# Plain additions for the softmax shift, and x loaded a second time in 32-channel pieces and transposed by VectorE instead of TensorE

## The chip, the core and the metric

The kernel runs on one core of a Trainium2 chip. The time is that of one execution on the device, in microseconds (us), the median of the executions shown. TensorE (PE) multiplies matrices out of SBUF into PSUM, VectorE (DVE), ScalarE (ACT) and GpSimd (POOL) work on 128 partitions by so many elements, and SyncE (SP) issues the transfers between memory and SBUF. Each engine runs its own instructions strictly in order; between engines, and where one instruction of an engine reads what the one before it wrote, there are semaphores.

## The reference

Self-attention over the W axis of an image tensor, after a normalisation with fixed mean and variance, everything in float32, B, H, W, C = 64, 128, 128, 64:

```
xn = (x - moving_mean) * rsqrt(moving_var + 0.001) * gamma + beta
q = xn @ Wq + bq;  k = xn @ Wk + bk;  v = xn @ Wv + bv
scores = einsum('bhid,bhjd->bhij', q, k) * 64 ** -0.5
attn = softmax(scores, axis=-1)
out = einsum('bhij,bhjd->bhid', attn, v) @ Wo + bo
return xn + out
```

There are 64 x 128 = 8192 rows of the image, each an attention of its own over 128 tokens of 64 channels.

## The kernel before

Eight image rows are a group; there are 1024 groups. The weights and the normalisation are folded once, at the start, into one 64x64 matrix for the scores (`w_g`), one for the output (`w_o`), a row of weights (`row_weights`, two rows of 64: one that scales x, one that gives the part of the score that depends on the query alone) and some biases (`const_bias` is one number per partition).

For each group n the work goes as follows, and the names are those of the tiles:

- SP loads x into `x_in` (128 tokens by 8 rows by 64 channels, 256 KB). There are eight buffers.
- PE transposes x (four 128x128 transposes into `ux_ps`, line 498) and DVE copies the result to `xT` (line 409), with channels of two image rows on the partitions. PE multiplies it with `w_g` (`g_ps`, line 483), ACT adds the bias (`g`, line 271), and PE makes the scores (`score_ps`, line 456).
- POOL multiplies x with `row_weights` into `x_weighted` (line 231, 128x1024), which has two buffers, and adds a bias to one half of it: `x_scaled_rows` (line 236).
- DVE sums the other half of `x_weighted` over the channels (`row_const`, 8 numbers per partition, line 401). This is what lets POOL write its next `x_weighted` but one: POOL waits on `const_found` (n - 2).
- DVE finds the largest score of each row (`row_max`, line 376), then `top` = `row_const` + `const_bias` + `row_max` (line 392) and `neg_top` = `row_const` + `const_bias` - `top` (line 395), 8 numbers per partition each. Both use an instruction with two tiles and one per-partition number (SCALAR_TENSOR_TENSOR). ACT takes `neg_top` as the bias of the eight exponentials (`probs`, line 287).
- PE transposes `probs` in two halves (line 443), ACT copies them (`probsT`, lines 264 and 277), PE multiplies x with them (into `ux_ps`, the same PSUM bank as the x transposes, line 467), DVE copies that to `uT` (line 385), PE multiplies by `w_o` (`o_ps`, line 508), and DVE multiplies with one over the sum of the exponentials (`inv_sum` line 365, `attn` line 370).
- POOL adds `attn` and `x_scaled_rows` (`y`, line 245) and SP stores `y`.

The work is pipelined by hand. In step t each engine takes different groups, always in the same written order:

- DVE: `inv_sum` and `attn` of group t-3, `row_max` of t, `uT` of t-2, `top` and `neg_top` of t, `row_const` of t+1, `xT` of t+2.
- POOL: `x_weighted` and `x_scaled_rows` of t+2, `y` of t-3.
- PE: scores of t, the product with x of t-2, first half of the transposed `probs` of t-1, `g_ps` of t+1, second half, the x transposes of t+2, `o_ps` of t-2.
- SP: the load of t+4, the store of t-3.

POOL's wait, in its step for group n = t+2, is this:

```
if exists(r, n - 2, peeled):
    pool.wait_ge(const_found[parts(n - 2)], uses(r, n - 2))
    pool.wait_ge(x_scaled[parts(n - 2)], uses(r, n - 2))
```

The steady part is a loop of eight steps per turn (`Fori`), with 19 steps written out ahead of it and 12 behind it.

Of the kernel before, what the change touches and what calls it, by code (L numbers as in the profile page):

```python
# [6 lines left out]
ALU = mybir.AluOpType  # L7
# [10 lines left out]
def build(nc: bass.Bass, x, gamma, beta, mean, var, wq, bq, wk, bk, wv, bv, wo, bo, out):  # L18
# [7 lines left out]
    x_groups = x.rearrange("b h w c -> (b h) w c").rearrange("(g s) w c -> g w s c", s=GROUP)  # L26
    out_groups = out.rearrange("b h w c -> (b h) w c").rearrange("(g s) w c -> g w s c", s=GROUP)

    with ExitStack() as ctx:
# [13 lines left out]
        x_in = sb("x_in", [128, 8, GROUP, C])  # L43
        xT = sb("xT", [128, 4, PAIRS, W])
        g = sb("g", [128, 4, PAIRS, W])
        x_weighted = sb("x_weighted", [128, 2, GROUP, 2, C])
        x_scaled_rows = sb("x_scaled_rows", [128, 8, GROUP, C])
        row_const = sb("row_const", [128, 4, GROUP])
# [36 lines left out]
        ux_ps, g_ps, probsT_ps, o_ps = (psum(n) for n in ("ux_ps", "g_ps", "probsT_ps", "o_ps"))  # L85
        score_ps = [psum(f"score_ps{i}", (128, 2, 512)) for i in range(2)]

        x_loaded = sem_ring("x_loaded", 8)
        y_stored = sem_ring("y_stored")
        xT_made = sem_ring("xT_made")  # L90
# [11 lines left out]
        neg_top_found = sem_ring("neg_top_found")  # L102
        const_found = sem_ring("const_found")
# [20 lines left out]
        class Turn:  # L124


            def __init__(self, eng, r, dma):
                self.r = r
                self.uses = {k: eng.snap(r * 2 + k) for k in range(-2, 5)}
                self.dma = {k: eng.snap((r * 2 + k) * DMA_INC) for k in range(-2, 5)} if dma else {}  # L130
                self.dma8 = {k: eng.snap((r + k) * DMA_INC) for k in range(0, 3)} if dma else {}
# [5 lines left out]
        def dma_uses(r, n):  # L137
            k = n // SEMS + 1
            return DMA_INC * (2 * r + k) if isinstance(r, int) else r.dma[k]

# [26 lines left out]
        def _(sp):  # L167
# [16 lines left out]

            def store(r, n, peeled):
# [4 lines left out]

            load(0, 0, True)

            def step(r, t, peeled):
                load(r, t + 4, peeled)
                store(r, t - 3, peeled)
# [15 lines left out]
        def _(pool):  # L211
# [38 lines left out]
        def _(act):  # L250
# [6 lines left out]
            def step(r, t, peeled):  # L257
# [21 lines left out]
                if exists(r, n, peeled):  # L279
# [6 lines left out]
                    for q in range(GROUP):  # L286
                        last = nc.scalar.activation(probs[:, n % 2, q, :], score_ps[n % 2][:, q % 2, q // 2 * W:(q // 2 + 1) * W],  # L287
# [9 lines left out]
        def _(dve):  # L297
# [50 lines left out]
            for h in range(2):  # L348
                p = slice(h * C, (h + 1) * C)
                chain(nc.vector.tensor_copy(w_g[p, h, :], ux_ps[p, 0:C]))  # L350
                chain(nc.vector.tensor_copy(w_o[p, h, :], ux_ps[p, C:2 * C]))
            chain(nc.vector.tensor_copy(row_weights[:, 1, :], ux_ps[:, 2 * C:3 * C]))
            chain(nc.vector.tensor_tensor(out_bias[:], ux_ps[:, 3 * C:4 * C], b_row[:], ALU.add))
            chain(nc.vector.tensor_copy(g_bias[:], ux_ps[:, 4 * C:4 * C + 1]))
            chain(nc.vector.tensor_copy(const_bias[:], ux_ps[:, 4 * C + 1:4 * C + 2]))
# [4 lines left out]
            def step(r, t, peeled):  # L360
# [12 lines left out]
                if exists(r, n, peeled):  # L373
                    s = parts(n)
                    dve.wait_ge(scores_made[s], uses(r, n))
                    nc.vector.tensor_reduce(row_max[:, s, :].rearrange("p (k h) -> p h k", h=2),  # L376
# [3 lines left out]
                if exists(r, n, peeled):  # L380
# [4 lines left out]
                    nc.vector.tensor_copy(uT[:, n % 2], ux_ps[:].rearrange("p (k w) -> p k w", k=PAIRS)) \  # L385
                        .then_inc(u_kept[s], 1)
                n = t
                if exists(r, n, peeled):
# [23 lines left out]
            pipeline(dve, step)  # L412

        @block.tensor
        def _(pe):
# [12 lines left out]
            for o, lhsT, rhs in ((0, wqT, w_foldT[:, 1, 0, :]),  # L428
# [5 lines left out]
                last = nc.tensor.matmul(ux_ps[:, o:o + rhs.shape[1]], lhsT, rhs, start=True, stop=True)  # L434
# [4 lines left out]
            w_o_all = w_o[:].rearrange("p h c -> p (h c)")  # L439

# [5 lines left out]
            def step(r, t, peeled):  # L446
# [13 lines left out]
                if exists(r, n, peeled):  # L460
                    s = parts(n)
                    pe.wait_ge(probsT_b_kept[s], uses(r, n))
                    if exists(r, n + 3, peeled):
                        pe.wait_ge(xT_kept[parts(n + 3)], uses(r, n + 3))
                    for k in range(PAIRS):
                        for h in range(2):
                            last = nc.tensor.matmul(ux_ps[h * C:(h + 1) * C, k * W:(k + 1) * W], x_in[:, n % 8, 2 * k + h, :],  # L467
                                                    probsT[:, n % 2, 2 * k + h, :], start=True, stop=True)
# [22 lines left out]
                n = t + 2  # L491
                if exists(r, n, peeled):
                    s = parts(n)
                    pe.wait_ge(x_loaded[n % 8], load_uses(r, n))
# [38 lines left out]
```

## Time and profile before

| | us |
|---|---|
| median of 3 executions | 5887.01 (5886.72 to 5887.08) |
| the profiled execution, its own time | 5891.6 |
| its span in the trace | 5889.8 |

| engine | busy us | share of the span |
|---|---|---|
| DVE | 5769.4 | 98% |
| PE | 5650.5 | 96% |
| POOL | 4992.3 | 85% |
| ACT | 4783.0 | 81% |
| the 16 DMA engines, mean | | 41.6% |

TensorE's granted clock is 0.999 of full speed over the span. An instruction counts as busy from its start to its end in the trace, whatever it does or waits for in between; idle time ahead of an instruction is shown apart, with what released it. In the timeline a row gives start, duration, engine, line, operation, output and inputs, and in brackets the idle time ahead of it.

### The profile page before, as it was taken

How to read it: one execution, taken by the hardware profiler on the slowest of the kernel's cores; microseconds unless marked ns; L12 is line 12 of the kernel's file. 1: busy time of each engine (PE TensorE's matmuls, PEld its weight loads, DVE VectorE, ACT ScalarE, POOL GpSimd, SP SyncE). 2: the span in 40 equal slices, each digit the busy share in tenths (PEclk: the TensorE clock that was granted, in tenths of full speed). 3: DMA queues.
4: the chain of work that ended last, by engine and by line, in shares of the span. 5: the costliest groups of instructions: out<-in, count | busy, mean ns of one | idle time of the engine just before them, and what ended most of it. 6: DMA issues, size and time to landing. Idle time of an engine off the chain costs nothing.

```text
span 5889.8 us, 169868 instructions
## 1 busy us (share of the span) xinstructions
PE 5650.5 (96%) x55320; PEld 4441.6 (75%) x55320; DVE 5769.4 (98%) x8226; ACT 4783.0 (81%) x19460; POOL 4992.3 (85%) x3080
## 2 busy tenths in 40 slices
PE   7999999999999999999999999999999999999999
PEld 6777777777777777777777777777777777777777
DVE  8999999999999999999999999999999999999999
ACT  6888888888888888888888888888888888888887
POOL 7888888888888888888888888888888888888887
PEclk9999999999999999999999999999999999999999
DMA  3444444444444444444444444444444444444443
GB/s 76 91 93 93 92 91 91 93 93 91 91 92 93 93 91 91 93 93 92 91 91 93 93 91 91 92 93 93 91 91 92 93 92 91 91 93 93 91 91 85
DMA packets 2131546, 537.56 MB, mean 91 GB/s; under 512 B 2131520, under 2 KB 2131520, under 8 KB 2131520
## 3 DMA queue, kind: packets, MB, share of 16 engines
q1 hardware_dynamic: 2131520, 537.23, 41.6%
q8 instruction: 14, 0.23, 0.0%
q14 instruction: 12, 0.10, 0.0%
HBM read 268.67 MB, written 268.44 MB: 91 GB/s over the span
## 4 chain that ended last, share of the span: by engine, by line
PE 68%; DVE 23%; issue 8%; DVEq 1%; POOL 0%; SPq 0%; ACT 0%; DMA 0%; POOLq 0%
PE probsT_ps L443 17%; PE ux_ps L467 17%; PE o_ps L508 14%; PE g_ps L483 13%; DVE xT L409 11%; DVE row_const L401 8%; PE ux_ps L498 7%; DVE top L392 2%; DVE uT L385 1%; DVE row_max L376 1%; DVEq L369 1%; DVEq L156 0%; DVE inv_sum L365 0%; PE score_ps L456 0%; POOL y L245 0%
## 5 line engine op out<-in xcount | busy, mean ns | idle before, releaser
L287 ACT ACTIVATE probs<-score_ps,neg_top 128x128 f32<-128x128 f32 x8192 | 2874.9, 376 | 686.1 <-DVE neg_top L395 686.1
L231 POOL TENSOR_TENSOR x_weighted<-x_in,row_weights 128x1024 f32<-128x1024 f32 x1024 | 2427.1, 2370 | 789.1 <-issue 675.9
L287 ACT ACTIVATION_READ_ACCUMULATOR probs<-score_ps,neg_top 128x1 f32 x8192 | 1765.5, 216 | 0.0
L443 PEld LDWEIGHTS probsT_ps<-ident,probs 128*128 128x128 f32 x8192 | 859.0, 140 | 915.0 <-issue 727.4
L236 POOL TENSOR_TENSOR x_scaled_rows<-x_weighted,out_bias 128x512 f32<-128x512 f32 x1024 | 1307.4, 1277 | 90.8 <-POOL x_weighted L231 20.2
L443 PE MATMUL probsT_ps<-ident,probs 128*128 128x128 f32 x8192 | 1315.5, 283 | 5.9 <-ACT probs L287 3.7
L467 PE MATMUL ux_ps<-probsT,x_in 128*64 128x128 f32 x16384 | 1120.8, 278 | 203.1 <-DVE xT L409 176.7
L245 POOL TENSOR_TENSOR y<-attn,x_scaled_rows 128x512 f32<-128x512 f32 x1024 | 1301.6, 1271 | 13.8 <-DVE attn L370 13.8
L395 DVE SCALAR_TENSOR_TENSOR neg_top<-row_const,const_bias,top 128x8 f32<-128x8 f32 x1024 | 1217.1, 1189 | 36.3
L376 DVE TENSOR_REDUCE row_max<-score_ps 128x8 f32<-128x1024 f32 x1024 | 1243.4, 1214 | 2.2 <-PE score_ps L456 2.0
L456 PE MATMUL score_ps<-xT,g 64*128 64x128 f32 x16384 | 1190.0, 285 | 0.3 <-ACT g L271 0.3
L467 PEld LDWEIGHTS ux_ps<-probsT,x_in 128*64 128x64 f32 x16384 | 895.9, 136 | 376.2 <-issue 300.9
L456 PEld LDWEIGHTS score_ps<-xT,g 64*128 64x128 f32 x16384 | 993.9, 187 | 124.2 <-ACT g L271 1.1
L508 PE MATMUL o_ps<-w_o,uT 128*128 128x128 f32 x8192 | 1082.1, 275 | 0.8 <-DVE uT L385 0.8
L483 PE MATMUL g_ps<-xT,w_g 128*128 128x512 f32 x2048 | 1050.3, 595 | 0.9 <-DVE xT L409 0.9
L508 PEld LDWEIGHTS o_ps<-w_o,uT 128*128 128x128 f32 x8192 | 995.3, 192 | 1.0 <-DVE uT L385 1.0
L271 ACT ACTIVATE g<-g_ps,g_bias 128x512 f32<-128x512 f32 x1024 | 703.8, 687 | 290.4 <-PE g_ps L483 290.3
L392 DVE SCALAR_TENSOR_TENSOR top<-row_const,const_bias,row_max 128x8 f32<-128x8 f32 x1024 | 816.6, 798 | 0.1
L370 DVE TENSOR_TENSOR attn<-o_ps,inv_sum 128x512 f32<-128x512 f32 x1024 | 707.9, 691 | 53.0 <-issue 5.7
L264 ACT ACTIVATE probsT<-probsT_ps 128x512 f32<-128x512 f32 x1024 | 611.5, 597 | 107.3 <-PE probsT_ps L443 3.0
L385 DVE COPY uT<-ux_ps 128x512 f32<-128x512 f32 x1024 | 696.8, 680 | 0.6 <-PE ux_ps L467 0.6
L409 DVE COPY xT<-ux_ps 128x512 f32<-128x512 f32 x1024 | 690.8, 675 | 3.8 <-PE ux_ps L498 3.8
(66 smaller groups left out, 2908.1 us busy)
## 6 DMA issues: line engine op xcount, KB each, us to landing
x_in<-in_x SPq DMA_DIRECT2D x1024, 256.0 KB, 3.2
out<-y SPq DMA_DIRECT2D x1024, 256.0 KB, 2.8
norm_row<-in_L_conv_gamma SPq DMA_DIRECT2D x1, 32.0 KB, 3.7
norm_row<-in_L_conv_beta SPq DMA_DIRECT2D x1, 32.0 KB, 3.7
norm_row<-in_L_conv_moving_mean SPq DMA_DIRECT2D x1, 32.0 KB, 4.2
norm_row<-in_L_conv_moving_var SPq DMA_DIRECT2D x1, 32.0 KB, 4.3
norm_row<-in_L_conv_bo SPq DMA_DIRECT2D x1, 32.0 KB, 4.5
w_raw<-in_L_conv_Wq SPq DMA_DIRECT2D x1, 16.0 KB, 1.9
```

The lines of the kernel that those rows point to most:

```text
L231: nc.gpsimd.tensor_tensor(x_weighted[:, n % 2], x_in[:, n % 8, :, None, :].broadcast_to([128, GROUP, 2, C]), weights_b, ALU.mult).then_inc ...
L236: nc.gpsimd.tensor_tensor(x_scaled_rows[:, n % 8], x_weighted[:, n % 2, :, 0, :], bias_b, ALU.add).then_inc(x_scaled[s], 1)
L245: nc.gpsimd.tensor_tensor(y[:, s], attn[:, s], x_scaled_rows[:, n % 8], ALU.add).then_inc(y_found[s], 1)
L287: last = nc.scalar.activation(probs[:, n % 2, q, :], score_ps[n % 2][:, q % 2, q // 2 * W:(q // 2 + 1) * W], ACT.Exp, bias=neg_top[:, s, q ...
L376: nc.vector.tensor_reduce(row_max[:, s, :].rearrange("p (k h) -> p h k", h=2), score_ps[n % 2][:].rearrange("p h (k w) -> p h k w", k=PAIR ...
L395: nc.vector.scalar_tensor_tensor(neg_top[:, s, :], row_const[:, s, :], const_bias[:, 0:1], top[:, s, :], ALU.add, ALU.subtract).then_inc(n ...
L409: nc.vector.tensor_copy(xT[:, s], ux_ps[:].rearrange("p (k w) -> p k w", k=PAIRS)) \
L443: last = nc.tensor.transpose(probsT_ps[:, (q - first) * W:(q - first + 1) * W], probs[:, n % 2, q, :], ident[:])
L456: last = nc.tensor.matmul(score_ps[n % 2][:, h, k * W:(k + 1) * W], g[half, s, k, :], xT[half, s, k, :], start=True, stop=True)
L467: last = nc.tensor.matmul(ux_ps[h * C:(h + 1) * C, k * W:(k + 1) * W], x_in[:, n % 8, 2 * k + h, :], probsT[:, n % 2, 2 * k + h, :], start ...
L483: nc.tensor.matmul(g_ps[:], w_g_all, xT[:, s].rearrange("p k w -> p (k w)"), start=True, stop=True).then_inc(g_made[s], 1)
L508: last = nc.tensor.matmul(o_ps[:, k * 2 * C:(k + 1) * 2 * C], uT[:, n % 2, k, :], w_o_all, start=True, stop=True)
```

## The change

Three things are changed together.

1. `top` and `neg_top` become plain additions of two tiles. For this `const_bias` is added beforehand: DVE's sum over the channels now writes `row_part`, and a new DVE instruction, at the end of the step, makes `row_const` = `row_part` + `const_bias` (8 numbers per partition). POOL now waits on `row_part` (`part_found`), where it waited on `row_const`.
2. x is read from memory a second time. For each group SP issues four more transfers, each of 32 partitions with 16 runs of 32 channels (128 bytes) per partition, 64 KB each, into a new tile `x_quads`. They go ahead of the load of `x_in`.
3. DVE transposes `x_quads` in 32x32 blocks into `xT`, in the place where it copied `xT` out of PSUM. The four x transposes on PE and their waits go away; the PSUM bank is now used by the product with x alone (`u_ps`). The pairs of rows that share a tile are now (k, k+4) in place of (2k, 2k+1), so the order of indices on PE, ACT and DVE's `row_max` changes with it.

```diff
 POOL, step for n = t + 2:
-                        pool.wait_ge(const_found[parts(n - 2)], uses(r, n - 2))
+                        pool.wait_ge(part_found[parts(n - 2)], uses(r, n - 2))

 SP:
+            def load_quads(r, n, peeled):
+                if not exists(r, n, peeled):
+                    return
+                s = parts(n)
+                if exists(r, n - 4, peeled):
+                    sp.wait_ge(xT_kept[s], uses(r, n - 4))
+                for h in range(2):
+                    for a in range(2):
+                        q = 32 * (2 * h + a)
+                        sp.dma_start(x_quads[q:q + 32, s].rearrange("p k (b c) -> p (k b) c", c=32),
+                                     x_blocks[group(r, n), h, a]).then_inc(quads_loaded[s], DMA_INC)
...
             def step(r, t, peeled):
+                load_quads(r, t + 4, peeled)
                 load(r, t + 4, peeled)
                 store(r, t - 3, peeled)

 DVE, step:
-                    nc.vector.scalar_tensor_tensor(top[:, s, :], row_const[:, s, :], const_bias[:, 0:1], row_max[:, s, :],
-                                                   ALU.add, ALU.add).then_inc(top_found[s], 1)
+                    nc.vector.tensor_tensor(top[:, s, :], row_const[:, s, :], row_max[:, s, :],
+                                            ALU.add).then_inc(top_found[s], 1)
                     dve.wait_ge(top_found[s], uses(r, n))
-                    nc.vector.scalar_tensor_tensor(neg_top[:, s, :], row_const[:, s, :], const_bias[:, 0:1], top[:, s, :],
-                                                   ALU.add, ALU.subtract).then_inc(neg_top_found[s], 1)
+                    nc.vector.tensor_tensor(neg_top[:, s, :], row_const[:, s, :], top[:, s, :],
+                                            ALU.subtract).then_inc(neg_top_found[s], 1)
                 n = t + 1
...
                     dve.wait_ge(x_weighed[s], uses(r, n))
-                    nc.vector.tensor_reduce(row_const[:, s, :], x_weighted[:, n % 2, :, 1, :],
-                                            AX_X, ALU.add).then_inc(const_found[s], 1)
+                    nc.vector.tensor_reduce(row_part[:, s, :], x_weighted[:, n % 2, :, 1, :],
+                                            AX_X, ALU.add).then_inc(part_found[s], 1)
                 n = t + 2
...
-                    dve.wait_ge(xT_made[s], uses(r, n))
+                    dve.wait_ge(quads_loaded[s], quad_uses(r, n))
                     if exists(r, n - 4, peeled):
                         dve.wait_ge(scores_made[s], uses(r, n - 4))
-                    nc.vector.tensor_copy(xT[:, s], ux_ps[:].rearrange("p (k w) -> p k w", k=PAIRS)) \
-                        .then_inc(xT_kept[s], 1)
+                    nc.vector.transpose(xT[:, s].rearrange("p k w -> p (k w)"),
+                                        x_quads[:, s].rearrange("p k w -> p (k w)")).then_inc(xT_kept[s], 1)
+                n = t + 1
+                if exists(r, n, peeled):
+                    s = parts(n)
+                    dve.wait_ge(part_found[s], uses(r, n))
+                    nc.vector.tensor_tensor(row_const[:, s, :], row_part[:, s, :], const_bias[:, 0:1].broadcast_to([128, GROUP]),
+                                            ALU.add).then_inc(const_found[s], 1)

 PE, product with x of t - 2, and the x transposes:
-                    if exists(r, n + 3, peeled):
-                        pe.wait_ge(xT_kept[parts(n + 3)], uses(r, n + 3))
+                    if exists(r, n - 1, peeled):
+                        pe.wait_ge(u_kept[parts(n - 1)], uses(r, n - 1))
...
-                    for k in range(PAIRS):
-                        last = nc.tensor.transpose(ux_ps[:, k * W:(k + 1) * W],
-                                                   x_in[:, n % 8, 2 * k:2 * k + 2, :].rearrange("p s c -> p (s c)"), ident[:])
-                    last.then_inc(xT_made[s], 1)
```

The order of instructions on VectorE, one step of the steady part, before (from `row_const` to `neg_top`; sizes are partitions by elements):

```order
L401 TENSOR_REDUCE row_const<-x_weighted 128x8
L409 COPY xT<-ux_ps 128x512
L365 RECIPROCAL inv_sum<-prob_sum 128x8
L370 TENSOR_TENSOR attn<-o_ps,inv_sum 128x512
L376 TENSOR_REDUCE row_max<-score_ps 128x2x4
L385 COPY uT<-ux_ps 128x512
L392 SCALAR_TENSOR_TENSOR top<-row_const,const_bias,row_max 128x8
L395 SCALAR_TENSOR_TENSOR neg_top<-row_const,const_bias,top 128x8
```

And the same place after the change:

```order
L425 TENSOR_REDUCE row_part<-x_weighted 128x8
L433 STREAM_TRANSPOSE xT<-x_quads 128x512
L439 TENSOR_TENSOR row_const<-row_part,const_bias 128x8
L389 RECIPROCAL inv_sum<-prob_sum 128x8
L394 TENSOR_TENSOR attn<-o_ps,inv_sum 128x512
L400 TENSOR_REDUCE row_max<-score_ps 128x8
L409 COPY uT<-u_ps 128x512
L416 TENSOR_TENSOR top<-row_const,row_max 128x8
L419 TENSOR_TENSOR neg_top<-row_const,top 128x8
```

The step has nine instructions where it had eight: `row_const` is now a small instruction of its own behind the transpose, and ahead of `inv_sum`.

On TensorE the same step, before:

```order
L456 MATMUL score_ps<-xT,g 128x128 x8
L467 MATMUL ux_ps<-probsT,x_in 64x128 x8
L443 MATMUL probsT_ps<-ident,probs 128x128 x4
L483 MATMUL g_ps<-xT,w_g 128x512
L443 MATMUL probsT_ps<-ident,probs 128x128 x4
L498 MATMUL ux_ps<-ident,x_in 128x128 x4
L508 MATMUL o_ps<-w_o,uT 128x128 x4
```

And after:

```order
L488 MATMUL score_ps<-xT,g 128x128 x8
L499 MATMUL u_ps<-probsT,x_in 64x128 x8
L475 MATMUL probsT_ps<-ident,probs 128x128 x4
L515 MATMUL g_ps<-xT,w_g 128x512
L475 MATMUL probsT_ps<-ident,probs 128x128 x4
L530 MATMUL o_ps<-w_o,uT 128x2x64 x4
```

Only the x transposes are gone; `o_ps` is written as two runs of 64.

## Rows read from the trace of the kernel before

**Rows 1.** The page: busy time by engine, and POOL's first group with its idle time.

```profile
PE 5650.5 (96%) x55320; PEld 4441.6 (75%) x55320; DVE 5769.4 (98%) x8226; ACT 4783.0 (81%) x19460; POOL 4992.3 (85%) x3080
...
L231 POOL TENSOR_TENSOR x_weighted<-x_in,row_weights 128x1024 f32<-128x1024 f32 x1024 | 2427.1, 2370 | 789.1 <-issue 675.9
```

**Rows 2.** The timeline of one steady step, VectorE and GpSimd: start, duration, engine.

```profile
3005.75 0.67 DVE L401 TENSOR_REDUCE row_const<-x_weighted 128x8 f32<-128x512 f32 x1
...
3006.35 0.68 DVE L409 COPY xT<-ux_ps 128x512 f32<-128x512 f32 x1
...
3006.56 2.37 POOL L231 TENSOR_TENSOR x_weighted<-x_in,row_weights 128x1024 f32<-128x1024 f32 x1 [0.75 <-issue]
...
3006.95 0.19 DVE L365 RECIPROCAL inv_sum<-prob_sum 128x8 f32<-128x8 f32 x1
...
3007.17 0.69 DVE L370 TENSOR_TENSOR attn<-o_ps,inv_sum 128x512 f32<-128x512 f32 x1
...
3007.78 1.21 DVE L376 TENSOR_REDUCE row_max<-score_ps 128x8 f32<-128x1024 f32 x1
...
3008.91 0.68 DVE L385 COPY uT<-ux_ps 128x512 f32<-128x512 f32 x1
3009.00 1.27 POOL L236 TENSOR_TENSOR x_scaled_rows<-x_weighted,out_bias 128x512 f32<-128x512 f32 x1
3009.50 0.80 DVE L392 SCALAR_TENSOR_TENSOR top<-row_const,const_bias,row_max 128x8 f32<-128x8 f32 x1
...
3010.23 1.27 POOL L245 TENSOR_TENSOR y<-attn,x_scaled_rows 128x512 f32<-128x512 f32 x1
...
3010.34 1.19 DVE L395 SCALAR_TENSOR_TENSOR neg_top<-row_const,const_bias,top 128x8 f32<-128x8 f32 x1
...
3011.45 0.67 DVE L401 TENSOR_REDUCE row_const<-x_weighted 128x8 f32<-128x512 f32 x1
```

**Rows 3.** Lines 395 and 392 alone: ns min/median/max, first and last start.

```profile
L395 DVE SCALAR_TENSOR_TENSOR neg_top<-row_const,const_bias,top x1024: 227/1192/1310, 37.1 to 5875.1; 128x8 f32<-128x8 f32 x171
...
L392 DVE SCALAR_TENSOR_TENSOR top<-row_const,const_bias,row_max x1024: 217/802/2254, 34.8 to 5874.8; 128x8 f32<-128x8 f32 x171
```

**Rows 4.** The timeline of the first steps, around the first `top`.

```profile
34.70 2.35 POOL L231 TENSOR_TENSOR x_weighted<-x_in,row_weights 128x1024 f32<-128x1024 f32 x1
...
34.82 2.25 DVE L392 SCALAR_TENSOR_TENSOR top<-row_const,const_bias,row_max 128x8 f32<-128x8 f32 x1
...
37.13 1.26 POOL L236 TENSOR_TENSOR x_scaled_rows<-x_weighted,out_bias 128x512 f32<-128x512 f32 x1
```

**Rows 5.** The timeline of the last steps; GpSimd's next row after this `y` starts at 5872.81.

```profile
5868.74 1.26 POOL L245 TENSOR_TENSOR y<-attn,x_scaled_rows 128x512 f32<-128x512 f32 x1 [2.13 <-DVE attn L370]
...
5870.30 0.22 DVE L392 SCALAR_TENSOR_TENSOR top<-row_const,const_bias,row_max 128x8 f32<-128x8 f32 x1
...
5870.56 0.23 DVE L395 SCALAR_TENSOR_TENSOR neg_top<-row_const,const_bias,top 128x8 f32<-128x8 f32 x1
5870.70 0.68 DVE L401 TENSOR_REDUCE row_const<-x_weighted 128x8 f32<-128x512 f32 x1
```

**Rows 6.** The timeline of the same steady step as Rows 2, TensorE.

```profile
3007.17 1.09 PE L467 MATMUL ux_ps<-probsT,x_in 128*64 128x128 f32 x16 [0.23 <-DVE xT L409]
...
3010.10 0.60 PE L498 MATMUL ux_ps<-ident,x_in 128*128 128x128 f32 x4
...
3010.53 1.06 PE L508 MATMUL o_ps<-w_o,uT 128*128 128x128 f32 x8
```

**Rows 7.** The page on transfers: packets and bytes, then the queue's share of 16 engines.

```profile
DMA packets 2131546, 537.56 MB, mean 91 GB/s; under 512 B 2131520, under 2 KB 2131520, under 8 KB 2131520
...
q1 hardware_dynamic: 2131520, 537.23, 41.6%
```

**Rows 8.** The timeline of SP at the start: the first eight loads, issued in a burst.

```profile
10.16 9.06 SPq L183 DMA_DIRECT2D x_in<-in_x  x8
```

**Rows 9.** Who waited for whom, SP: us in total, times, longest.

```profile
SPq L189 <- POOL y L245: 4591.6, 1024, 34.1
```

More of the change, by code:

```diff
@@ L43, in build @@
         x_in = sb("x_in", [128, 8, GROUP, C])
+        x_quads = sb("x_quads", [128, 4, PAIRS, W])
         xT = sb("xT", [128, 4, PAIRS, W])
@@ L47, in build @@
         x_scaled_rows = sb("x_scaled_rows", [128, 8, GROUP, C])
+        row_part = sb("row_part", [128, 4, GROUP])
         row_const = sb("row_const", [128, 4, GROUP])
@@ L81, in build @@
         row_tmp = sb("row_tmp", [128, 3, C])
-        ux_ps, g_ps, probsT_ps, o_ps = (psum(n) for n in ("ux_ps", "g_ps", "probsT_ps", "o_ps"))
+        u_ps, g_ps, probsT_ps, o_ps = (psum(n) for n in ("u_ps", "g_ps", "probsT_ps", "o_ps"))
         score_ps = [psum(f"score_ps{i}", (128, 2, 512)) for i in range(2)]
         x_loaded = sem_ring("x_loaded", 8)
+        quads_loaded = sem_ring("quads_loaded")
         y_stored = sem_ring("y_stored")
-        xT_made = sem_ring("xT_made")
         g_made = sem_ring("g_made")
@@ L130, in __init__ @@
                 self.dma = {k: eng.snap((r * 2 + k) * DMA_INC) for k in range(-2, 5)} if dma else {}
+                self.quads = {k: eng.snap((r * 2 + k) * 4 * DMA_INC) for k in range(-2, 5)} if dma else {}
                 self.dma8 = {k: eng.snap((r + k) * DMA_INC) for k in range(0, 3)} if dma else {}
@@ L139, in dma_uses, with quad_uses @@
             return DMA_INC * (2 * r + k) if isinstance(r, int) else r.dma[k]
+        def quad_uses(r, n):
+            k = n // SEMS + 1
+            return 4 * DMA_INC * (2 * r + k) if isinstance(r, int) else r.quads[k]
         def load_uses(r, n):
@@ L349, in _ @@
                 p = slice(h * C, (h + 1) * C)
[L350 to L355, printed above, removed]
+                chain(nc.vector.tensor_copy(w_g[p, h, :], u_ps[p, 0:C]))
+                chain(nc.vector.tensor_copy(w_o[p, h, :], u_ps[p, C:2 * C]))
+            chain(nc.vector.tensor_copy(row_weights[:, 1, :], u_ps[:, 2 * C:3 * C]))
+            chain(nc.vector.tensor_tensor(out_bias[:], u_ps[:, 3 * C:4 * C], b_row[:], ALU.add))
+            chain(nc.vector.tensor_copy(g_bias[:], u_ps[:, 4 * C:4 * C + 1]))
+            chain(nc.vector.tensor_copy(const_bias[:], u_ps[:, 4 * C + 1:4 * C + 2]))
             assert done[0] == DVE_READY, done[0]
@@ L375, in step @@
                     dve.wait_ge(scores_made[s], uses(r, n))
-                    nc.vector.tensor_reduce(row_max[:, s, :].rearrange("p (k h) -> p h k", h=2),
+                    nc.vector.tensor_reduce(row_max[:, s, :].rearrange("p (h k) -> p h k", h=2),
                                             score_ps[n % 2][:].rearrange("p h (k w) -> p h k w", k=PAIRS),
@@ L433, in _ @@
                                  (4 * C + 1, bias_wide[:, 0, :], bias_fold[:, 1:2])):
-                last = nc.tensor.matmul(ux_ps[:, o:o + rhs.shape[1]], lhsT, rhs, start=True, stop=True)
+                last = nc.tensor.matmul(u_ps[:, o:o + rhs.shape[1]], lhsT, rhs, start=True, stop=True)
             last.then_inc(pe_setup, 1)
@@ L439, in _ @@
             w_o_all = w_o[:].rearrange("p h c -> p (h c)")
+            o_pairs = o_ps[:].rearrange("p (h k c) -> p h k c", h=2, k=PAIRS)
             def transposed_probs(n, first):
@@ L462, in step @@
                     pe.wait_ge(probsT_b_kept[s], uses(r, n))
-                    if exists(r, n + 3, peeled):
-                        pe.wait_ge(xT_kept[parts(n + 3)], uses(r, n + 3))
+                    if exists(r, n - 1, peeled):
+                        pe.wait_ge(u_kept[parts(n - 1)], uses(r, n - 1))
                     for k in range(PAIRS):
                         for h in range(2):
-                            last = nc.tensor.matmul(ux_ps[h * C:(h + 1) * C, k * W:(k + 1) * W], x_in[:, n % 8, 2 * k + h, :],
-                                                    probsT[:, n % 2, 2 * k + h, :], start=True, stop=True)
+                            last = nc.tensor.matmul(u_ps[h * C:(h + 1) * C, k * W:(k + 1) * W], x_in[:, n % 8, PAIRS * h + k, :],
+                                                    probsT[:, n % 2, PAIRS * h + k, :], start=True, stop=True)
                     last.then_inc(u_made[s], 1)
@@ L507, in step @@
                     for k in range(PAIRS):
-                        last = nc.tensor.matmul(o_ps[:, k * 2 * C:(k + 1) * 2 * C], uT[:, n % 2, k, :], w_o_all,
+                        last = nc.tensor.matmul(o_pairs[:, :, k, :], uT[:, n % 2, k, :], w_o_all,
                                                 start=True, stop=True)
```

15 lines of the change are left out of this document (6 added, 9 removed).

## The prediction

> **What bounds the kernel now.** The page first: DVE 98% and PE 96% busy, POOL 85% [rows 1]. That reads as a VectorE bound, but POOL sat idle 789.1 us ahead of `x_weighted`, 0.77 us in each of 1024 steps, always in the same place. So I read one steady step of DVE and POOL side by side [rows 2].
>
> `x_weighted` starts at 3006.56, 0.14 us after `row_const` has ended (3006.42). `x_scaled_rows` follows at 3009.00 and `y` at 3010.23, ending at 3011.50. And DVE's `top`, 8 numbers per partition, takes 0.80 us and ends at 3010.30, where `x_scaled_rows` ends (3010.27); `neg_top` takes 1.19 us and ends at 3011.53, where `y` ends (3011.50). Over all steps they took 217 to 2254 and 227 to 1310 ns [rows 3]. Where POOL is idle they take 0.22 and 0.23 us [rows 5]. The very first `top` met a just started `x_weighted`: begun 0.12 us after it, it ended at 37.07, that instruction at 37.05 [rows 4]. So a DVE instruction that reads two SBUF tiles waits until the POOL instruction in progress has ended; it gets through at the boundary between two. Instructions with one SBUF input don't: `row_const`, `inv_sum`, `attn` (its other input is PSUM) and `uT` run at their usual length beside POOL's.
>
> That closes a loop: `row_const` lets POOL start; three POOL instructions follow; `y` holds `neg_top`, and `row_const` of the next step is queued behind `neg_top`. With T the start of `row_const`: x_weighted +0.81, x_scaled_rows +3.25, y +4.48 to +5.75, next `row_const` +5.70 [rows 2]. The mean over the kernel, first to last `neg_top`, is (5875.1 - 37.1) / 1023 = 5.707 us [rows 3]. PE is not in this loop: it waits 0.23 us for DVE's `xT` in that step [rows 6].
>
> **The change, part by part**, on that clock, T now being the start of `row_part`.
>
> *POOL's release.* `row_part` is the same reduction in the same place, and POOL now waits on it. `x_weighted` again starts at +0.81 and ends at +3.18 (2.37 long). The release is not moved.
>
> *The transpose* starts at +0.60 like the copy did. The trace has no such instruction. Nearest rows: the sum over the same 128x512 out of SBUF, 0.67 us, and the copy of 128x512, 0.68 us. I take 0.68; below, nothing suggests under 0.3; above, four passes over the data would be 2.7. Up to about 2.4 us it costs nothing, because of what comes next.
>
> *The new addition* reads `row_part` and `const_bias`, both in SBUF, and is DVE's third instruction of that kind in a step. It would start at +1.20 (+0.60 + 0.60), inside `x_weighted` (+0.81 to +3.18). By [rows 4] it waits to the end: done at +3.21, and what follows on DVE starts at +3.13 (0.08 before the end, as `row_const` did behind `neg_top` in [rows 2]). What is queued behind it: `inv_sum`, `attn`, `row_max`, `uT`, `top`. The Trainium skill, page "SBUF — State Buffer", section "Who interferes with whom", states that a DVE instruction with two SBUF inputs contends with a GpSimd instruction that reads SBUF, and that plain tensor_tensor does too; this speaks against the change, since by it plain additions gain nothing and a third is one more wait. The trace agrees for the three-operand form (0.80 and 1.19 us against 0.22); for plain additions no row beside POOL shows it.
>
> *The rest of DVE's step*, by the distances between starts in [rows 2]: `inv_sum` +3.13, `attn` +3.35, `row_max` +3.96, `uT` +5.09, `top` +5.68. POOL meanwhile: `x_scaled_rows` +3.25, `y` +4.48 to +5.75 (`attn` is ready at +4.04). `top` meets the last 0.07 us of `y` and ends at +5.78; `neg_top` starts 0.04 later, +5.82, as in [rows 2]. POOL is idle, since it waits for the next `row_part`, so `neg_top` is short, and `row_part` starts 0.14 behind its start [rows 5]: **+5.96**.
>
> So the loop becomes `row_part`, `x_weighted`, the addition, and the whole of DVE's step, in place of POOL's three instructions. The waits of `top` and `neg_top` (0.58 and 0.96 us over 0.22) nearly vanish, and one of 1.9 us comes ahead of them.
>
> *PE* loses the x transposes, 0.43 us from their start to `o_ps` [rows 6]. It needs 5.70 - 0.23 - 0.43 = 5.04 us a step, below 5.96: no gain in time. Splitting `o_ps` into runs and the new pairs move no instruction; nothing.
>
> *Transfers.* 2048 packets of 256 bytes a step now; the first eight loads went out at 1.13 us each (9.06 / 8) [rows 8], so load and store need 2.3 us. The quads are 4 x 32 x 16 = 2048 packets of 128 bytes: 1.1 us if bytes count, 2.3 if packets do. Together 3.4 to 4.6 us of a 5.96 us step. The share of the DMA engines goes from 41.6% [rows 7] to between 60 and 80%. SP waits 4591.6 us of the span for `y` [rows 9] and has room for four more issues; the loads are asked for some three steps ahead. Cost nothing, as long as a step's packets stay below the step.
>
> **The sum.** (5.96 - 5.70) x 1023 = +266 us. The profiled execution's own time was 5891.6, 1.8 us more than its span of 5889.8 us; the median of the runs is 5887.0, 2.8 below that span. Span after: 6156; median: **6153 us**, 4.5% more. Its own uncertainty: `top` reaches POOL's `y` with 0.07 us to spare. If DVE is earlier nothing changes; if it is later by d, the loop grows by about d. With a free `neg_top` of 0.19 (like `inv_sum`) instead of 0.23, 5.92: 6112. With 0.15 us more on DVE, and register work of the loop that no longer hides, 6.15: 6347. Own range 6090 to 6350.
>
> **The rivals.**
>
> *Plain additions don't wait for POOL* (faster). For it: only the three-operand form is seen waiting. Against it: what the two forms have in common is two tiles from SBUF, and `attn`, a plain multiplication with one SBUF tile, never waits. Then DVE's step is 0.60 + 0.60 + 0.14 + 0.22 + 0.61 + 1.13 + 0.59 + 0.26 + 0.14 = 4.3, POOL's 4.94 (0.81 to 5.75), PE's 5.04 the longest: -0.66 x 1023, about 5210. It decides if `row_const` takes 0.2 us beside `x_weighted`. Chance 0.11.
>
> *Only the new addition slips through*, because its second operand is one number repeated and may not be fetched as a tile is. DVE then reaches `top` at 0.60 + 0.60 + 0.14 + 0.22 + 0.61 + 1.13 + 0.59 = +3.89, waits for `x_scaled_rows` to +4.55, `neg_top` for `y` to +5.78, and `row_part` starts at +5.70: the old loop to the last digit, 5887. Chance 0.09.
>
> *The transfers become the bound* (slower still). If a 128-byte packet cost twice a 256-byte one, 2.27 + 4.53 = 6.8 us a step, 5887 + 1.1 x 1023 = 7010. It decides from 29 ns a packet and engine ((5.96 - 2.27) x 16 / 2048) against 17.7 in the burst. For it: every packet is under 512 bytes already and these are smaller, scattered in memory; against: nothing in [rows 7] shows a price per byte missing. The Trainium skill, "DMA: Bandwidth & Descriptors", section "Why small descriptors are slow (HBM only)", gives a fixed cost per packet, 256/32 + 3 = 11 cycles at 256 bytes, so 7 at 128: by it the quads would take 7/11 of 2.27, an estimate of 1.4 us a step, and this rival would be out. Chance 0.05.
>
> **How the numbers follow.** The wait of the addition behind `x_weighted`: 0.75, and of that about 0.65 within 6090 to 6350. A range from 5870 to 6400 takes in the unchanged loop and leaves out the fast case and the transfers: about 0.8. Within 0.2% of before is about all that a measurement can tell from no change; faster 0.11, same 0.09, slower 0.80.
>
> **What would show it.** The new `row_const` near 1.9 to 2.0 us, ending with `x_weighted`; `top` near 0.1 to 0.3 and `neg_top` near 0.2 us; POOL idle about 1.0 us before each `x_weighted`; PE's share near 85%; DVE still near 98%; the transpose anywhere under 2.4 us without effect; the DMA share 60 to 80%. The prediction is wrong if `row_const` is short beside `x_weighted`, if DVE waits for `x_quads`, if the transpose exceeds 2.4 us, or if POOL's instructions themselves change length.

## The result

The changed kernel takes **6139.8 us** (median of 4, 6139.61 to 6140.16) against 5886.9 us before: ratio 1.043, 95% interval 1.042 to 1.044. It is slower by 253 us; 6153 us was forecast, and 6090 to 6350 as the forecast case's own range.

The page of the kernel after, busy time by engine and GpSimd's first group (beside [rows 1]):

```profile
span 6137.9 us, 172723 instructions
## 1 busy us (share of the span) xinstructions
PE 5404.5 (88%) x51224; PEld 4001.7 (65%) x51224; DVE 6021.7 (98%) x9250; ACT 4792.0 (78%) x19460; POOL 4974.4 (81%) x3080
...
L255 POOL TENSOR_TENSOR x_weighted<-x_in,row_weights 128x1024 f32<-128x1024 f32 x1024 | 2415.6, 2359 | 1054.5 <-issue 909.1
```

DVE is again 98% busy and PE is less so. GpSimd sits idle longer ahead of `x_weighted`, 1054.5 us against 789.1: 265 us more. GpSimd's own instructions took 18 us less in total (4974.4 against 4992.3), so the whole loss stands in this idle time.

The timeline of one steady step after, VectorE and GpSimd (beside [rows 2]):

```profile
3005.62 0.68 DVE L425 TENSOR_REDUCE row_part<-x_weighted 128x8 f32<-128x512 f32 x1
3006.22 0.70 DVE L433 STREAM_TRANSPOSE xT<-x_quads 128x512 f32<-128x512 f32 x1
...
3006.43 2.36 POOL L255 TENSOR_TENSOR x_weighted<-x_in,row_weights 128x1024 f32<-128x1024 f32 x1 [1.01 <-issue]
...
3006.84 1.97 DVE L439 TENSOR_TENSOR row_const<-row_part,const_bias 128x8 f32<-128x8 f32 x1
...
3008.74 0.19 DVE L389 RECIPROCAL inv_sum<-prob_sum 128x8 f32<-128x8 f32 x1
3008.87 1.27 POOL L260 TENSOR_TENSOR x_scaled_rows<-x_weighted,out_bias 128x512 f32<-128x512 f32 x1
3008.96 0.69 DVE L394 TENSOR_TENSOR attn<-o_ps,inv_sum 128x512 f32<-128x512 f32 x1
...
3009.57 1.21 DVE L400 TENSOR_REDUCE row_max<-score_ps 128x8 f32<-128x1024 f32 x1
...
3010.10 1.27 POOL L269 TENSOR_TENSOR y<-attn,x_scaled_rows 128x512 f32<-128x512 f32 x1
...
3010.70 0.68 DVE L409 COPY uT<-u_ps 128x512 f32<-128x512 f32 x1
3011.30 0.16 DVE L416 TENSOR_TENSOR top<-row_const,row_max 128x8 f32<-128x8 f32 x1
...
3011.49 0.17 DVE L419 TENSOR_TENSOR neg_top<-row_const,top 128x8 f32<-128x8 f32 x1
...
3011.57 0.68 DVE L425 TENSOR_REDUCE row_part<-x_weighted 128x8 f32<-128x512 f32 x1
```

From `row_part` to `row_part` it is 5.95 us, where it was 5.70. Read the addition of 8 numbers first: it starts inside `x_weighted`, takes 1.97 us, and ends at 3008.81, where `x_weighted` ends (3008.79). This is not this step alone: 1022 of the 1024 additions start inside an instruction of GpSimd, and each of them ends 19 to 45 ns after it. The other two took 124 and 167 ns. The rest of DVE's step follows the addition, and GpSimd, done with `y` at 3011.37, waits for the next `row_part`. `top` and `neg_top` show no wait any more: GpSimd is idle or just ending when they come.

The groups of VectorE after, mean ns of one after the busy time:

```profile
L439 DVE TENSOR_TENSOR row_const<-row_part,const_bias 128x8 f32<-128x8 f32 x1024 | 2005.9, 1959 | 0.0
...
L433 DVE STREAM_TRANSPOSE xT<-x_quads 128x512 f32<-128x512 f32 x1024 | 717.5, 701 | 0.0
...
L419 DVE TENSOR_TENSOR neg_top<-row_const,top 128x8 f32<-128x8 f32 x1024 | 172.6, 169 | 35.4
L416 DVE TENSOR_TENSOR top<-row_const,row_max 128x8 f32<-128x8 f32 x1024 | 159.6, 156 | 0.1
```

Line 419 alone: ns min/median/max, first and last start.

```profile
L419 DVE TENSOR_TENSOR neg_top<-row_const,top x1024: 166/166/2274, 34.4 to 6123.4; 128x8 f32<-128x8 f32 x171
```

And the transfers on the page after (beside [rows 7]):

```profile
DMA packets 4294236, 806.27 MB, mean 131 GB/s; under 512 B 4294208, under 2 KB 4294208, under 8 KB 4294208
## 3 DMA queue, kind: packets, MB, share of 16 engines
q1 hardware_dynamic: 4294208, 805.93, 65.4%
```

The page's chain, followed back from the last instruction, is VectorE's in the kernel after, and 29% of the span in it is `row_const` (line 439):

```profile
DVE 78%; issue 21%; DVEq 1%; PE 0%; POOL 0%; SPq 0%; DMA 0%; POOLq 0%; ACT 0%; ACTq 0%
```

### The profile page after: what moved, and what is told of

It is laid out like the page before. It is cut to its first block, busy times and chain, and to the rows that moved or that the text cites. A ratio compares the mean times of both kernels' runs of the same rounds, so it can differ in the third digit from the quotient of the medians.

```text
span 6137.9 us, 172723 instructions
## 1 busy us (share of the span) xinstructions
PE 5404.5 (88%) x51224; PEld 4001.7 (65%) x51224; DVE 6021.7 (98%) x9250; ACT 4792.0 (78%) x19460; POOL 4974.4 (81%) x3080
## 3 DMA queue, kind: packets, MB, share of 16 engines
q1 hardware_dynamic: 4294208, 805.93, 65.4%
## 4 chain that ended last, share of the span: by engine, by line
DVE 78%; issue 21%; DVEq 1%; PE 0%; POOL 0%; SPq 0%; DMA 0%; POOLq 0%; ACT 0%; ACTq 0%
DVE row_const L439 29%; DVE row_max L400 20%; DVE uT L409 10%; DVE row_part L425 7%; DVE xT L433 6%; DVE inv_sum L389 2%; DVE top L416 1%; DVE neg_top L419 1%; DVE attn L394 1%; DVEq L415 0%; DVEq L166 0%; POOL y L269 0%; DVEq L393 0%; DMA bias_col<-in_L_conv_bv 0%; PE u_ps L464 0%
## 5 line engine op out<-in xcount | busy, mean ns | idle before, releaser
L255 POOL TENSOR_TENSOR x_weighted<-x_in,row_weights 128x1024 f32<-128x1024 f32 x1024 | 2415.6, 2359 | 1054.5 <-issue 909.1
L439 DVE TENSOR_TENSOR row_const<-row_part,const_bias 128x8 f32<-128x8 f32 x1024 | 2005.9, 1959 | 0.0
L530 PE MATMUL o_ps<-w_o,uT 128*128 128x128 f32 x8192 | 1185.7, 288 | 700.0 <-DVE uT L409 700.0
L499 PE MATMUL u_ps<-probsT,x_in 128*64 128x128 f32 x16384 | 1120.5, 279 | 0.0
L499 PEld LDWEIGHTS u_ps<-probsT,x_in 128*64 128x64 f32 x16384 | 873.3, 136 | 124.1
L433 DVE STREAM_TRANSPOSE xT<-x_quads 128x512 f32<-128x512 f32 x1024 | 717.5, 701 | 0.0
L409 DVE COPY uT<-u_ps 128x512 f32<-128x512 f32 x1024 | 696.1, 680 | 0.6 <-PE u_ps L499 0.6
L425 DVE TENSOR_REDUCE row_part<-x_weighted 128x8 f32<-128x512 f32 x1024 | 694.0, 678 | 1.7 <-POOL x_weighted L255 1.7
```

The source lines that it names most:

```text
L255: nc.gpsimd.tensor_tensor(x_weighted[:, n % 2], x_in[:, n % 8, :, None, :].broadcast_to([128, GROUP, 2, C]), weights_b, ALU.mult).then_inc ...
L409: nc.vector.tensor_copy(uT[:, n % 2], u_ps[:].rearrange("p (k w) -> p k w", k=PAIRS)) \
L425: nc.vector.tensor_reduce(row_part[:, s, :], x_weighted[:, n % 2, :, 1, :], AX_X, ALU.add).then_inc(part_found[s], 1)
L439: nc.vector.tensor_tensor(row_const[:, s, :], row_part[:, s, :], const_bias[:, 0:1].broadcast_to([128, GROUP]), ALU.add).then_inc(const_fo ...
L499: last = nc.tensor.matmul(u_ps[h * C:(h + 1) * C, k * W:(k + 1) * W], x_in[:, n % 8, PAIRS * h + k, :], probsT[:, n % 2, PAIRS * h + k, :] ...
L530: last = nc.tensor.matmul(o_pairs[:, :, k, :], uT[:, n % 2, k, :], w_o_all, start=True, stop=True)
```

## The experiments

Theory, as in the prediction: an instruction of VectorE with two tiles from SBUF waits until GpSimd's instruction in progress has ended, and the new addition stands where that costs about 1.8 us. Rivals: the second load or the transpose costs the time; or VectorE is simply full.

All times are medians. The ratio is to the kernel before, run on the same chip as the kernel of that row; from chip to chip its median lies between 5886.9 and 5890.2 us.

| kernel | us | ratio (95%) |
|---|---|---|
| only the load and the transpose (e1_quads_only) | 5875.7 | 0.998 (0.997 to 0.999) |
| only the additions (e2_adds_only) | 6145.4 | 1.044 (1.042 to 1.046) |
| the new addition ahead of the transpose (e3_add_early) | 5876.7 | 0.998 (0.997 to 0.999) |
| the new addition, one tile and a number (e4_add_scalar) | 6137.9 | 1.043 (1.041 to 1.044) |
| the same with a constant (e8_add_number) | 6137.4 | one run |
| two transposes (e9_two_transposes) | 6143.7 | 1.043 (1.041 to 1.045) |
| five transposes (e10_five_transposes) | 7534.1 | 1.279 (1.277 to 1.281) |
| reductions for additions (e7_pairs) | 5169.9 | 0.878 (0.877 to 0.880) |
| the same, x transposed on PE (e6_pairs_pe) | 5615.6 | 0.954 (0.952 to 0.955) |
| negated row_max, no additions (e5_negmax) | 5170.6 | 0.878 (0.877 to 0.880) |

**Each part alone.** The first kernel is the changed one with the old forms of `top` and `neg_top` and no third addition; `x_weighted` waits for the sum over the channels, as it did before. From its edit against the changed kernel:

```diff
-                    nc.vector.tensor_tensor(top[:, s, :], row_const[:, s, :], row_max[:, s, :],
-                                            ALU.add).then_inc(top_found[s], 1)
+                    nc.vector.scalar_tensor_tensor(top[:, s, :], row_const[:, s, :], const_bias[:, 0:1], row_max[:, s, :],
+                                                   ALU.add, ALU.add).then_inc(top_found[s], 1)
...
-                    nc.vector.tensor_tensor(row_const[:, s, :], row_part[:, s, :], const_bias[:, 0:1].broadcast_to([128, GROUP]),
-                                            ALU.add).then_inc(const_found[s], 1)
...
```

> Only the second load of x and the transpose on VectorE; top, neg_top and row_const are made as before. Theory (the wait of two-input instructions for GpSimd): the loop of row_const, three GpSimd instructions and the held neg_top is untouched, 5.70 us a step, 5887 us within 0.3%, although TensorE loses 0.43 us of work a step; transpose near 0.70 us. Rival (the load or the transpose costs the 4%): near 6140 us.

The second is the kernel before with only the additions changed: `top` and `neg_top` plain, `x_weighted` waiting on `row_part`, and the third addition behind the copy of `xT`. From its edit against the kernel before:

```diff
...
+                    nc.vector.tensor_tensor(row_const[:, s, :], row_part[:, s, :], const_bias[:, 0:1].broadcast_to([128, GROUP]),
+                                            ALU.add).then_inc(const_found[s], 1)
```

> Only the plain additions, with row_const as a third one behind the copy of xT; x is still transposed on TensorE and loaded once. Theory: the third addition waits about 1.97 us for x_weighted, 5.95 us a step, 6120 to 6150 us. Rival (the load or the transpose costs it): 5887 us.

5875.7 and 6145.4 us: the additions cost all of it, and the load, the transpose and PE's relief together cost nothing and give almost nothing. That also settles how to read the page of the kernel before, whose own chain lies mostly on PE:

```profile
PE 68%; DVE 23%; issue 8%; DVEq 1%; POOL 0%; SPq 0%; ACT 0%; DMA 0%; POOLq 0%
```

By that line PE would be the bound; yet with 0.43 us less for PE in each step, 440 us in all, the time fell by 12. The group of the addition in the second kernel:

```profile
L417 DVE TENSOR_TENSOR row_const<-row_part,const_bias 128x8 f32<-128x8 f32 x1024 | 2001.1, 1954 | 0.0
```

It takes the same 1.95 us, about 1.8 of it a wait, with no transpose and no second load there.

**The place of the addition.** In the changed kernel it moves from behind the transpose to directly behind `row_part`; nothing else changes.

```diff
                     nc.vector.tensor_reduce(row_part[:, s, :], x_weighted[:, n % 2, :, 1, :],
                                             AX_X, ALU.add).then_inc(part_found[s], 1)
+                    dve.wait_ge(part_found[s], uses(r, n))
+                    nc.vector.tensor_tensor(row_const[:, s, :], row_part[:, s, :], const_bias[:, 0:1].broadcast_to([128, GROUP]),
+                                            ALU.add).then_inc(const_found[s], 1)
```

> The changed kernel, with the addition that makes row_const moved directly behind row_part, ahead of the transpose. It then starts about 0.10 us before GpSimd's x_weighted. Theory: it slips in ahead (0.15 us), top waits for x_scaled_rows and neg_top for y again, 5.70 to 5.77 us a step, 5885 to 5960 us. If GpSimd is in first all the same, the addition waits for all of x_weighted: 5.95 to 6.05 us a step, 6140 to 6240. Rival (an extra instruction costs what it costs, wherever it stands): 6140 us.

5876.7 us, just under the 5885 to 5960 expected: the whole loss is undone by where the addition stands. The timeline of its steady step:

```profile
3002.07 1.27 POOL L269 TENSOR_TENSOR y<-attn,x_scaled_rows 128x512 f32<-128x512 f32 x1
3002.17 1.19 DVE L419 TENSOR_TENSOR neg_top<-row_const,top 128x8 f32<-128x8 f32 x1
...
3003.29 0.67 DVE L425 TENSOR_REDUCE row_part<-x_weighted 128x8 f32<-128x512 f32 x1
...
3003.99 0.17 DVE L428 TENSOR_TENSOR row_const<-row_part,const_bias 128x8 f32<-128x8 f32 x1
...
3004.09 2.36 POOL L255 TENSOR_TENSOR x_weighted<-x_in,row_weights 128x1024 f32<-128x1024 f32 x1 [0.75 <-issue]
```

It starts 0.10 us ahead of `x_weighted` and takes 0.17 us. The old loop is back: the plain `neg_top` takes 1.19 us and ends with `y` (3003.36 against 3003.34), just as the three-operand one did. The trace of before had no such row, a plain addition with two tiles waiting for GpSimd.

**Which forms wait.** The addition with one tile and a per-partition number, and then with the constant 0.0 in the place of that number (this one leaves `const_bias` out of the sum). The edit of the first:

```diff
-                    nc.vector.tensor_tensor(row_const[:, s, :], row_part[:, s, :], const_bias[:, 0:1].broadcast_to([128, GROUP]),
-                                            ALU.add).then_inc(const_found[s], 1)
+                    nc.vector.tensor_scalar(row_const[:, s, :], row_part[:, s, :], const_bias[:, 0:1], None,
+                                            ALU.add).then_inc(const_found[s], 1)
```

> The changed kernel, with the addition that makes row_const written as one tile plus a per-partition number (tensor_scalar). If only a second tile from SBUF waits for GpSimd: the addition takes 0.15 to 0.2 us, top and neg_top wait in its place, 5.70 us a step, 5880 to 5900 us. If the per-partition number or a faster mode of this instruction needs the shared side as well: 1.97 us, 6140 us.

> The changed kernel with the new addition as one tile plus a constant written in the instruction, 0.0, so const_bias is left out of it. If the per-partition number was what waited for GpSimd in the form with one tile, the addition takes 0.15 to 0.2 us and the time is near 5877; if a tile read and written in SBUF with this instruction is enough, it waits 1.97 us again and the time is near 6138.

6137.9 and 6137.4 us. Its line in the two kernels: ns min/median/max.

```profile
L439 DVE TENSOR_SCALAR row_const<-row_part,const_bias x1024: 186/1977/2336, 30.8 to 6117.2; 128x8 f32<-128x8 f32 x171
```

```profile
L439 DVE TENSOR_SCALAR row_const<-row_part x1024: 129/1977/1986, 30.9 to 6116.8; 128x8 f32<-128x8 f32 x171
```

The wording "two SBUF tiles" was too narrow: this instruction has a single tile from SBUF and writes to SBUF, and waits just the same, with a per-partition number or with a constant. The Trainium skill, "SBUF — State Buffer", section "Who interferes with whom", says that copies and tensor_scalar can enter, when their operands meet certain conditions, a mode that takes both ports into SBUF and then contend with GpSimd. Both runs agree with it (1977 ns), though the mode itself is not seen in a trace. The Trainium skill says in the same section that tensor_reduce on trn2 never contends; the next kernels agree with that (129 to 170 ns).

**No such form at all.** Each small sum becomes a reduction over two neighbouring numbers of one tile. `trio` holds `row_max`, `row_const` and minus `top` side by side; `pair` holds the sum of `x_weighted` and `const_bias`. The arithmetic is the same. From the edit against the changed kernel:

```diff
-                    nc.vector.tensor_tensor(top[:, s, :], row_const[:, s, :], row_max[:, s, :],
-                                            ALU.add).then_inc(top_found[s], 1)
+                    nc.vector.tensor_reduce(trio[:, s, :, 2], trio[:, s, :, 0:2], AX_X, ALU.add, negate=True).then_inc(top_found[s], 1)
...
-                    nc.vector.tensor_tensor(neg_top[:, s, :], row_const[:, s, :], top[:, s, :],
-                                            ALU.subtract).then_inc(neg_top_found[s], 1)
+                    nc.vector.tensor_reduce(neg_top[:, s, :], trio[:, s, :, 1:3], AX_X, ALU.add).then_inc(neg_top_found[s], 1)
...
-                    nc.vector.tensor_tensor(row_const[:, s, :], row_part[:, s, :], const_bias[:, 0:1].broadcast_to([128, GROUP]),
-                                            ALU.add).then_inc(const_found[s], 1)
+                    nc.vector.tensor_reduce(trio[:, s, :, 1], pair[:, s], AX_X, ALU.add).then_inc(const_found[s], 1)
```

> The changed kernel with the same sums, but each small addition is a reduction over two neighbouring numbers of one tile, so that no instruction of VectorE's steady step has two inputs in SBUF. Theory: none of them waits for GpSimd (0.15 to 0.25 us each); the longest engine sets the step, TensorE at about 5.04 us with GpSimd at 4.94 close behind: 5.0 to 5.15 us, 5190 to 5320 us. Rival (these small instructions are slow for another reason than GpSimd, or VectorE is full): 5900 to 6140 us.

> The same reductions over two numbers, but x transposed on TensorE and loaded once, as before the change. Theory: no wait for GpSimd; TensorE, with the x transposes, is the longest engine at 5.47 us: 5640 to 5680 us. The difference to the kernel with the second load is then what taking the x transposes off TensorE is worth, 0.43 us a step or about 440 us. Rival: TensorE was never close to its limit, and both give the same time.

5169.9 us, 12% faster than before; with x transposed on PE and loaded once 5615.6. Both are a little under the lowest that was expected (5190 and 5640): PE's step without waits is 5.00 and 5.44 us, where 5.04 and 5.47 were taken. The page of the first of them, and its groups of VectorE:

```profile
PE 5133.4 (99%) x51224; PEld 3972.6 (77%) x51224; DVE 4239.4 (82%) x9251; ACT 4672.1 (90%) x19460; POOL 4990.8 (97%) x3080
...
q1 hardware_dynamic: 4294208, 805.93, 78.9%
...
PE 99%; issue 0%; DVE 0%; POOL 0%; ACT 0%; SPq 0%; DMA 0%; POOLq 0%; DVEq 0%; ACTq 0%
```

```profile
L417 DVE TENSOR_REDUCE neg_top<-trio 128x8 f32<-128x16 f32 x1024 | 174.1, 170 | 35.6
L415 DVE TENSOR_REDUCE trio<-trio 128x8 f32<-128x16 f32 x1024 | 162.7, 159 | 0.1
L436 DVE TENSOR_REDUCE trio<-pair 128x8 f32<-128x16 f32 x1024 | 132.2, 129 | 0.0
```

And the place of the third sum in its steady step:

```profile
3003.36 2.37 POOL L253 TENSOR_TENSOR x_weighted<-x_in,row_weights 128x1024 f32<-128x1024 f32 x1
...
3003.77 0.13 DVE L436 TENSOR_REDUCE trio<-pair 128x8 f32<-128x16 f32 x1
```

The three sums take 129 to 170 ns each, with GpSimd 97% busy beside them. The third starts 0.41 us into `x_weighted`, just where the addition of the changed kernel started, and is done long before it ends. VectorE falls from 98% busy to 82% with as many instructions in the step; the chain that ended last is 99% PE. The difference between the two kernels, 445.7 us or 0.436 us a step, is PE's time for the x transposes [rows 6]: the second half of the change does pay, once the wait for GpSimd is gone.

**Less work for VectorE.** `neg_top` straight from the reduction, without `top` and without the new addition; the part of the shift that depends on the query alone is left out, since it cancels in the softmax:

```diff
-                    nc.vector.tensor_reduce(row_max[:, s, :].rearrange("p (h k) -> p h k", h=2),
+                    nc.vector.tensor_reduce(neg_top[:, s, :].rearrange("p (h k) -> p h k", h=2),
                                             score_ps[n % 2][:].rearrange("p h (k w) -> p h k w", k=PAIRS),
-                                            AX_X, ALU.max).then_inc(max_found[s], 1)
+                                            AX_X, ALU.max, negate=True).then_inc(neg_top_found[s], 1)
```

> The changed kernel without top and without the new addition: neg_top is the negated row_max, straight from the reduction (the part that depends on the query alone cancels in the softmax; row_part is still summed and still releases GpSimd). VectorE has 0.5 us less to do than with the reductions over two numbers. Theory: TensorE is the limit, so the same time within 1%, 5190 to 5320 us. Rival (VectorE is the limit there): 0.3 to 0.5 us a step less than that kernel.

5170.6 us, the same, and again just under the 5190 expected. VectorE is no bound there; PE is.

**More work for VectorE.** The transpose twice, and five times, the extra ones into a spare tile and ahead of the one into `xT`. The loop of the second kernel; in the first it is `range(1)`:

```diff
+                    for i in range(4):
+                        nc.vector.transpose(spare[:, i, :], x_quads[:, s].rearrange("p k w -> p (k w)"))
```

> The changed kernel with the transpose done a second time, into a spare tile: 0.62 us more for VectorE in each step. Theory: the addition behind it arrives at +1.84 us, still inside x_weighted (+0.81 to +3.17), waits 0.62 us less, and nothing changes: 6140 us within 0.3%. Rival (VectorE, 98% busy, is the bound by its work): 0.62 x 1023 more, 6770 us.

> The transpose five times, four into a spare tile: 2.48 us more for VectorE in each step. Theory: the addition arrives at +3.70 us, after x_weighted and inside x_scaled_rows (+3.25 to +4.52), so it ends at +4.55 in place of +3.20; the step grows by about 1.34 us, to 7.29 us, 7510 us. Had only the time beyond x_weighted's end counted, 0.5 us, 6650. Rival (all of the added work counts): 8.43 us a step, 8680 us.

6143.7 us: 0.62 us of work more in each step, and 4 us in all; the kernel before, too, took 3 us more on that chip (5890.2 against 5886.9), and the ratio is the same 1.043. An engine that is 98% busy had 0.6 us to spare, inside the addition that waits, whose mean fell from 1959 to 1375 ns:

```profile
L444 DVE TENSOR_TENSOR row_const<-row_part,const_bias 128x8 f32<-128x8 f32 x1024 | 1407.8, 1375 | 0.0
```

With five it is 7534.1 us, where following the addition from one instruction of GpSimd to the next gave 7510 and the plain sum of all added work 8680. The timeline:

```profile
3006.34 2.48 DVE L437 STREAM_TRANSPOSE spare<-x_quads 128x512 f32<-128x512 f32 x4
3006.56 2.36 POOL L256 TENSOR_TENSOR x_weighted<-x_in,row_weights 128x1024 f32<-128x1024 f32 x1 [1.39 <-issue]
3008.75 0.67 DVE L438 STREAM_TRANSPOSE xT<-x_quads 128x512 f32<-128x512 f32 x1
3009.00 1.27 POOL L261 TENSOR_TENSOR x_scaled_rows<-x_weighted,out_bias 128x512 f32<-128x512 f32 x1
3009.34 0.95 DVE L444 TENSOR_TENSOR row_const<-row_part,const_bias 128x8 f32<-128x8 f32 x1
...
3011.30 1.26 POOL L270 TENSOR_TENSOR y<-attn,x_scaled_rows 128x512 f32<-128x512 f32 x1 [1.02 <-DVE attn L395]
```

The addition now misses the end of `x_weighted` (3008.92) by 0.42 us, starts 0.34 us into `x_scaled_rows` and waits for its end (3010.27): late by a little, it pays for the rest of the next instruction of GpSimd. The transposes, a tile read and written in SBUF like the tensor_scalar above, don't wait: the four extra ones take 2.48 us together, most of it inside `x_weighted`, and 677 ns each on average over the kernel.

## Why the prediction was right

The time and the mechanism were both right for the change as it was made. One general sentence of the prediction was wrong, and two small errors in the step cancelled; both are below.

- **The loop that bounds the kernel.** Shown. Taking the waits away (the reductions) left PE as the bound, at 5.00 and 5.44 us a step, and DVE's 98% became 82%.
- **The new addition waits behind `x_weighted`.** Forecast to end at +3.21 of the step; it ended at +3.19 (3008.81 - 3005.62). Its place alone carries the loss.
- **What waits, and what doesn't.** "Instructions with one SBUF input don't" was wrong as a rule: the tensor_scalar has one and waits 1.8 us. It did no harm here, since none of DVE's steady instructions before or after the change is of that form. Why some forms wait is not shown by any run. All the waiting instructions had 8 numbers per partition, and all of GpSimd's read SBUF; larger ones, or a GpSimd instruction that only writes, were not tried.
- **The rest of the step.** Forecast `inv_sum` +3.13, `attn` +3.35, `row_max` +3.96, `uT` +5.09, `top` +5.68, next `row_part` +5.96. Measured +3.12, +3.34, +3.95, +5.08, +5.68, +5.95. The forecast had `top` held to the end of `y` and done at +5.78, `neg_top` starting at +5.82, and `row_part` 0.14 behind it. In fact `top` took the 0.16 us that it takes anyway (0.15 in the kernel with five transposes, where GpSimd is idle then) and ended at +5.84, past the end of `y` at +5.75, so no wait shows; `neg_top` started at +5.87, and `row_part` only 0.08 behind it. One error of 0.05 us and one of 0.06 cancelled: that the step came out within 0.01 us is in part luck.
- **The sum.** 253 us for 266. By the first and last `neg_top` the mean step went from 5.707 us to (6123.4 - 34.4) / 1023 = 5.952, so it grew by 0.245 us. The prediction took 0.26, because it subtracted the one step's 5.70 and not its own mean of 5.707, and had 5.96 for 5.952.
- **The transpose.** Taken as 0.68, measured 0.70; free up to about 2.4 us was forecast. Twice the transpose (1.24 us) was free, five times (3.1) was not; where between them it ends was not measured.
- **The transfers.** Forecast share 60 to 80%, measured 65.4%. By share x 16 x span / packets a packet took 18.4 ns of one DMA engine before; the added 2.16 million took (0.654 x 6137.9 - 0.416 x 5889.8) x 16 / 2162688 = 11.6 ns each. Only 2097152 of them are the quads' own packets of 128 bytes; if the others took no time, it is 11.9 ns. Half the bytes cost 0.63 to 0.65 of the time, so that rival was far off: 29 ns would have been needed. The Trainium skill, "DMA: Bandwidth & Descriptors", section "Why small descriptors are slow (HBM only)", has a fixed cost per packet, and the prediction's estimate from it was 7/11 = 0.64. The trace agrees.
- **Plain additions don't wait** (the faster rival): refuted by the plain `neg_top` of 1.19 us (the addition placed early) and the `row_const` of 1.97. Its price was sound: 5210 us with PE as the bound, and 5170 in the kernels where nothing waits. **Only the new one slips through**: refuted by the same `row_const`.
- **The signs.** PE's share was forecast near 85% and is 88%. GpSimd's instructions were to keep their length: `x_weighted` went from 2370 to 2359 ns, which is 11 us of the whole and the other way than the loss. The rest of the list came as forecast.
- **PE's relief is worth nothing here.** Shown for this loop (5875.7 us with it alone). The 0.2% by which that kernel and the one with the early addition beat the kernel before was not forecast. `x_weighted` is 9 and 6 ns shorter a step in them (2361 and 2364 against 2370), which is 9 of 12 us in the one and 6 of 11 in the other; why it is shorter stays open.

## What to carry to other kernels

Where a tiny instruction of one engine ends, step after step, with a large one of its neighbour, most of its time is a wait, and "busy" includes it: read two engines side by side before believing a share. In this kernel such a wait was set by where the instruction stands and by its form: an addition of 8 numbers with two SBUF tiles, or a tensor_scalar from SBUF to SBUF, that starts 0.4 us into a 2.4 us instruction of GpSimd waits out the other 2 us, while a reduction in the same place takes 0.13 us. A relief for one engine (here PE's x transposes) is worth what the loop through the others lets it be: nothing at first, 0.44 us a step after the waits were gone.

## What was not expected of the hardware

A tensor_scalar on 8 numbers with a constant waits for GpSimd as long as an addition of two tiles does (1977 ns median, against 129 at its shortest). A transpose of 128x512 in 32x32 blocks, from SBUF to SBUF, doesn't: in the kernel with two of them the second lies wholly inside `x_weighted` in 1022 steps and took 665 to 672 ns there.

TensorE's granted clock was 0.933 of full speed over the span with five transposes, against 1.0 in the changed kernel. In the trace it is at its lower level, 1.2 GHz, for 1007 of 7532 us, in many short stretches, and at 2.4 GHz for the rest. What differs is PE's idle time ahead of `o_ps`, 1.9 us in one piece in most steps where it was 0.68:

```profile
3005.61 1.16 PE L535 MATMUL o_ps<-w_o,uT 128*128 128x128 f32 x8 [1.89 <-DVE uT L410]
```

This `o_ps` ran at the higher level; another, at 509.48, with the same 1.88 us of idle time ahead of it, took 1.85 us at the lower one. Which steps fall stays open. The time does not show it: the steps with such a stretch in them are no longer than the others (median 7.30 and 7.31 us).
